# A recurrence in units of 16 value columns instead of 8, and every queue in a new order

## The chip, the cores and the metric

One core of one Trainium2 chip. The time is device microseconds of one execution, from launch to the last result. The kernel before was timed in 3 runs: median 1855.06 us, from 1853.09 to 1856.74.

## The reference

Two layers over 32 independent batches of 128 x 512 float32. The first is an attention over channels: two instance norms, two 128 x 128 projections, a softmax of 512 x 512, its product with a projection of the second input, and a residual. The second is a block in the manner of RWKV; its core is a scan over 128 time steps, in 32 heads of 16 x 16 state. It reads `x` (32 x 128 x 512) and a context of the same shape, whose rows also give the state at the start.

```
Mn = Wn @ inorm(x_c) + bn ; Mm = Wm @ inorm(x_s) + bm
A  = softmax(Mn^T Mm) ; y = Wo (Wl x_s + bl) A^T + bo + x_c
xa = ln(y) ; sx = shift(xa) - xa ; five mixes -> w, r, k, v, g
def step(s, (r_t, k_t, v_t, w_t)):
    a   = k_t[..., :, None] * v_t[..., None, :]
    out = einsum('bhi,bhij->bhj', r_t, u * a + s)
    s   = a + w_t[..., :, None] * s
x1 = y + groupnorm(out) * silu(g) @ Wo.T
out = x1 + sigmoid(xr2 @ Wfr.T) * (relu(xk2 @ Wfk.T)**2 @ Wfv.T)
```

## The kernel before, in words

Everything is float32. There is one instruction queue for each engine, written by hand: `opening()`, then `step(on)` for s = 5 to 30 (26 times, written out, not a loop on the chip), then `closing()`. A step works on five batches at once: `b0` in the attention (`att_*`), `b1` in the mixes and projections (`mid_*`), `b2` in the recurrence (`wkv_*`), `b3` in the head norm and first residual (`tail_*`), `b4` in the last products (`fin_*`). Engines meet only by semaphores; `Steps` (L53) counts labels, so the order of labels in L228 to L254 is the order in each engine's queue. TensorE's results go through rings of PSUM banks (L86 to L91): a job gets the next bank of its ring and waits, in `bank_free` (L276), for the reader of the job that had the bank last. Bank 4 (`SUM_BANK`) collects the recurrence, bank 5 (`O_BANK`) the transposed result.

The recurrence (L855 to L889) is computed for pairs of time steps. Partition = one key row of a head (128 of 512 in each of C = 4 chunks), free axis = value columns x time. A unit is one chunk and `UJ` = 8 of the 16 value columns; there are `U` = 8 units a batch. In each:

- SP loads `vrep` (`load_vrep`, L331): v of the unit, replicated over the 16 key rows of its head, from the DRAM tensor `v_dram`, 512 KB. ScalarE has stored v there (`mid_v`, L1560). `vrep` has two buffers.
- VectorE: `wkv_outer` (L862) A = vrep * kt, 8 x 126; `wkv_pair` (L868) adds each pair of A into S, 8 x 63; `wkv_scan` (L877) runs the scan over S with decays `wrep`, 8 x 64; `wkv_read` (L889) A = S * rt, each state read twice, 8 x 128. A and S have two buffers.
- GpSimd puts the state at the start into column 0 of S (`wkv_s0`, L543). Its other large jobs are the five adds of the mixes (`mid_add`, L516), `rku` and `rk2`, the power -0.5 of the head norm (`rstd_of`, L489) and the last add (`fin_out`, L556).
- TensorE: `wkv_sum` (L2168): four products of A with 32 columns of ones, 256 columns each, over the keys; four units make half of the bank.

Four more places that the change touches. In the transpose of the tanh, `mid_Wt` (L2112), 64 columns of `txn` are turned, of which 32 are those of g. `tail_xc2` (L1642) writes two scaled copies of the second norm on ScalarE, one to be shifted by a time step, and `tail_mix` (L954) adds them. The last batch goes through the same code as all others. At the start, ScalarE and TensorE wait for 14 constants (`CONSTS`).

Of the kernel before, what the change touches and what calls it, by code (L numbers as in the profile page):

```python
# [29 lines left out]
UJ = 8  # L30
U = C * HS // UJ
# [47 lines left out]
def run(step):  # L79
# [7 lines left out]
    "O:1 V:0 Tx:1 W1:1 Mn:0 Wt:1 Mm:0 Mv:1 Mw:1 S0:0 S1:0 S2:0 Vp:1 Mk:1 Mr:1 Mg:1 D1:1 S3:0 Kp:1 "  # L87
    "D2:1 E2:1 Rp:1 T0:0 T1:0 T2:0 G:1 T3:0").split())]
BACK_JOBS = [(j, int(lag)) for j, lag in (x.split(":") for x in (
    "FK:4 C:3 C2:3 FR:4 FV:4 Tg:3 Wo:3 Tx2:3").split())]  # L90
# [3 lines left out]
def build(nc, x_c, x_s, state, params, att_w, big_w, maa_w1, maa_w2, td_w1, td_w2, out, v_dram):  # L94
    with ExitStack() as ctx:
# [26 lines left out]
        w2g = sb("w2g", [2 * DM, E])  # L122
# [14 lines left out]
        rsum = sb("rsum", [P, C])  # L137
        rinv = sb("rinv", [P, C])
# [6 lines left out]
        xx = sb("xx", [P, C, P])  # L145
        tx = sb("tx", [P, P])
        txg = sb("txg", [2 * DM, P])
# [9 lines left out]
        wrep = sb("wrep", [P, C, UJ, T2])  # L157
# [10 lines left out]
        pv = sb("pv", [P, C, T2])  # L168
# [15 lines left out]
        kk = sb("kk", [P, C, P])  # L184
# [17 lines left out]
        xhat2 = sq  # L202

# [17 lines left out]
        act_setup = sem("act_setup")  # L221
        wv_centred = sem("wv_centred")
# [5 lines left out]
        dve_att = Steps(sem("dve_att"), "stats aggr nm mx0 mx1 mx2 ri1 ri0 mx3 ri2 ri3 xin xst xag nm1")  # L228
        dve_mid = Steps(sem("dve_mid"), "sx xx s0m mv mw mk mr mg s0c g")
        dve_pre = Steps(sem("dve_pre"), "kw rw")  # L230
        dve_outer = Steps(sem("dve_outer"), units("a"))
# [5 lines left out]
        act_att = Steps(sem("act_att"), "v xn yn Mn Mm p1 p2 p0 n0 n1 p3 n2 n3 T0 T1 T2 T3 xhat")  # L237
        act_mid = Steps(sem("act_mid"), "xa tn tx vT dt ez k dw r th")
# [59 lines left out]
        def _(sp):  # L298
            regs = [sp.alloc_register(f"sync_wait{i}") for i in range(2)]
            sp.dma_start(xc[:, 0, :], x_c[0]).then_inc(x_loaded[0], 16)  # L300
            sp.dma_start(xs[:, 0, :], x_s[0]).then_inc(x_loaded[0], 16)
            sp.dma_start(attw[:, :, :], att_w).then_inc(setup_loaded[0], 16)
            sp.dma_start(par[:, :], params).then_inc(setup_loaded[0], 16)
# [101 lines left out]
            def closing():  # L405
# [2172 lines left out]
```

## Time and profile before

| what | value |
|---|---|
| median of 3 runs | 1855.06 us |
| the profiled execution, its own time | 1854.93 us |
| its span, first to last instruction | 1853.2 us |
| TensorE busy | 1774.6 us, 96% |
| VectorE busy | 1744.8 us, 94% |
| ScalarE busy | 1176.3 us, 63% |
| GpSimd busy | 1015.3 us, 55% |
| chain that ended last | PE 50%, DVE 28%, issue 16%, DMA 2%, ACT 2% |
| TensorE clock, mean | 0.987 of 2.4 GHz |

In the profile PE is TensorE (PEld its weight loads, beside the matmuls), DVE VectorE, ACT ScalarE, POOL GpSimd, SP the engine that issues loads; a "q" behind a name is the engine's sequencer. `L877` is a line of the kernel. In a group's row come the line, engine, operation, result<-operands, shapes, the count, then busy us and mean ns of one, then idle time before it and what ended that. A float32 matmul is two records. Rows of the timeline begin with start and length in us; neighbours on an engine can overlap a little in the records.

### The profile page before, as it was taken

How to read it: one execution, taken by the hardware profiler on the slowest of the kernel's cores; microseconds unless marked ns; L12 is line 12 of the kernel's file. 1: busy time of each engine (PE TensorE's matmuls, PEld its weight loads, DVE VectorE, ACT ScalarE, POOL GpSimd, SP SyncE). 2: the span in 40 equal slices, each digit the busy share in tenths (PEclk: the TensorE clock that was granted, in tenths of full speed). 3: DMA queues.
4: the chain of work that ended last, by engine and by line, in shares of the span. 5: the costliest groups of instructions: out<-in, count | busy, mean ns of one | idle time of the engine just before them, and what ended most of it. 6: DMA issues, size and time to landing. Idle time of an engine off the chain costs nothing.

```text
span 1853.2 us, 35413 instructions
## 1 busy us (share of the span) xinstructions
PE 1774.6 (96%) x12420; PEld 1228.9 (66%) x12420; DVE 1744.8 (94%) x2468; ACT 1176.3 (63%) x2949; POOL 1015.3 (55%) x882
## 2 busy tenths in 40 slices
PE   5989999999999999999999999999999999999966
PEld 3666576667676667766676767666776667776743
DVE  3699999999999999999999999999999999999991
ACT  4666666666666767666667666676666666766523
POOL 1244465555665665566665566556566666554541
PEclk8999999999999999999999999999999999999978
DMA  6233434344333333433434333333343343433330
GB/s 246 72 90 96 104 85 101 89 106 105 96 88 99 99 92 104 107 91 91 104 88 107 106 97 87 98 99 93 104 108 91 90 104 86 118 96 77 93 82 18
DMA packets 81600, 180.98 MB, mean 98 GB/s; under 512 B 18288, under 2 KB 34800, under 8 KB 80400
## 3 DMA queue, kind: packets, MB, share of 16 engines
q1 hardware_dynamic: 59920, 161.93, 33.1%
q10 hardware_dynamic: 21504, 16.78, 2.8%
q8 instruction: 101, 1.65, 0.4%
q14 instruction: 75, 0.61, 0.1%
HBM read 161.91 MB, written 16.78 MB: 96 GB/s over the span
## 4 chain that ended last, share of the span: by engine, by line
PE 50%; DVE 28%; issue 16%; DMA 2%; ACT 2%; POOL 1%; DVEq 0%; ACTq 0%; POOLq 0%; SPq 0%
PE bank L2043 17%; PE bank L2050 6%; DVE A L862 6%; PE bank L2088 5%; DVE S L877 5%; PE bank L2055 4%; DVE A L889 3%; PE bank L2168 3%; DVE nmax L764 3%; DVE xf L820 3%; PE bank L2062 3%; DVE S L868 2%; PE bank L2075 2%; DMA vrep<-v_dram 2%; PE bank L2103 2%
## 5 line engine op out<-in xcount | busy, mean ns | idle before, releaser
L543 POOL COPY S<-s 128x8 f32<-128x8 f32 x256 | 190.3, 744 | 322.3 <-DVE A L889 231.6
L877 DVE TENSOR_TENSOR_SCAN S<-wrep,S 128x512 f32<-128x512 f32 x256 | 351.9, 1377 | 2.6 <-ACT wrep L1603 1.7
L889 DVE TENSOR_TENSOR A<-S,rt 128x1024 f32<-128x1024 f32 x256 | 327.5, 1283 | 0.4
L516 POOL TENSOR_TENSOR xf<-xf,xa 128x512 f32<-128x512 f32 x160 | 218.7, 1369 | 188.7 <-DVE xf L820 186.4
L862 DVE TENSOR_TENSOR A<-vrep,kt 128x1008 f32<-128x1008 f32 x256 | 310.8, 1218 | 7.4 <-DMA vrep<-v_dram 4.6
L1520 ACT ACTIVATE prob<-bank,nmax 128x512 f32<-128x512 f32 x128 | 87.4, 686 | 231.5 <-DVE nmax L764 231.5
L868 DVE TENSOR_TENSOR S<-A 128x504 f32<-128x504 f32 x256 | 225.8, 892 | 1.2
L489 POOL TENSOR_TENSOR hrs<-hrs,mhalf 128x32 f32<-128x32 f32 x32 | 198.7, 6211 | 2.7
L487 POOL TENSOR_SCALAR rstd<-mv 128x1 f32<-128x1 f32 (+1 forms) x96 | 72.8, 759 | 227.4 <-DVE mv L784 141.2
L1557 ACT ACTIVATE bank<-bank,par 128x128 f32<-128x128 f32 x640 | 174.6, 352 | 29.0 <-PE bank L2124 29.0
L2168 PE MATMUL bank<-A,slide 128*32 128x256 f32 x2048 | 163.4, 394 | 13.8 <-DVE A L889 13.4
L2075 PE MATMUL bank<-probT 128*128 128x512 f32 x256 | 132.1, 619 | 5.5 <-ACT prob L1520 2.4
L2043 PEld LDWEIGHTS bank<-xk,Wfk 128*128 128x128 f32 x1024 | 121.5, 198 | 19.5 <-DVE xk L954 18.8
L2043 PE MATMUL bank<-xk,Wfk 128*128 128x128 f32 x1024 | 127.4, 285 | 5.5 <-DVE xk L954 5.4
L1651 ACT ACTIVATE xp<-bank,prev 128x128 f32<-128x128 f32 x256 | 130.4, 509 | 0.0
L2050 PE MATMUL bank<-Wo,ogT 128*128 128x512 f32 x256 | 121.8, 620 | 7.8 <-DVE ogT L931 6.4
L2043 PEld LDWEIGHTS bank<-xf,Wr 128*128 128x128 f32 x1024 | 116.7, 192 | 18.9 <-POOL xf L516 16.2
L2043 PE MATMUL bank<-xf,Wr 128*128 128x128 f32 x1024 | 121.9, 277 | 5.3 <-ACT prob L1520 5.3
L2043 PEld LDWEIGHTS bank<-xf,Wv 128*128 128x128 f32 x1024 | 116.9, 192 | 14.3 <-POOL xf L516 11.9
L2043 PEld LDWEIGHTS bank<-xf,Wk 128*128 128x128 f32 x1024 | 116.8, 192 | 14.0 <-issue 12.1
L2043 PE MATMUL bank<-xf,Wv 128*128 128x128 f32 x1024 | 122.6, 278 | 0.7 <-POOL xf L516 0.7
L2043 PE MATMUL bank<-xf,Wk 128*128 128x128 f32 x1024 | 122.5, 278 | 0.3
(143 smaller groups left out, 3890.8 us busy)
## 6 DMA issues: line engine op xcount, KB each, us to landing
vrep<-v_dram SPq DMA_DIRECT2D x256, 512.0 KB
xc<-x_c SPq DMA_DIRECT2D x32, 256.0 KB, 6.2
xs<-x_s SPq DMA_DIRECT2D x32, 256.0 KB, 9.4
v_dram<-vT ACTq DMA_DIRECT2D x32, 256.0 KB, 7.2
out<-rr ACTq DMA_DIRECT2D x32, 256.0 KB, 6.4
st<-state SPq DMA_DIRECT2D x64, 2.0 KB, 6.4
Wv<-big_w SPq DMA_DIRECT2D x1, 1024.0 KB, 7.2
Wk<-big_w SPq DMA_DIRECT2D x1, 1024.0 KB, 9.2
```

Source lines behind the costliest of these rows:

```text
L489: po.tensor_tensor(rs, rs, mhalf[:, 0:rs.shape[1]], ALU.pow).then_inc(own.sem, 1)
L516: po.tensor_tensor(xf[:, b, :, :], xf[:, b, :, :], xa[:, :, 1:P + 1], ALU.add).then_inc(pool_mid.sem, 1)
L543: po.tensor_copy(S[:, u % 2, :, 0], s0[:, p, k:k + UJ]).then_inc(pool_wkv.sem, 1)
L862: ve_.tensor_tensor(A[:, u % 2, :, 0:P - 2], vrep[:, u % 2, :, 0:P - 2], k, ALU.mult).then_inc(dve_outer.sem, 1)
L868: ve_.tensor_tensor(S[:, u % 2, :, 1:T2], first(a), second(a), ALU.add).then_inc(dve_pair.sem, 1)
L877: ve_.tensor_tensor_scan(s, wrep[:, u % C, :, :].rearrange("p j t -> p (j t)"), s, 0.0, ALU.mult, ALU.add).then_inc(dve_scan.sem, 1)
L889: ve_.tensor_tensor(out4, s, r, ALU.mult).then_inc(dve_read.sem, 1)
L1557: last = sc.activation(ps, ps, ACT.Identity, bias=col("maa_stack", c, MIX.index(f)))
L2043: last = pe.matmul(ps[:, o * P:(o + 1) * P], w[:, c, o * P:(o + 1) * P], src[:, c, :], start=(c == 0), stop=(c == C - 1))
L2050: last = pe.matmul(bank_of(job)[:, :], src[:, c, :], w[:, c, :], start=(c == 0), stop=(c == C - 1))
L2075: pe.matmul(bank_of(f"S{t}")[:, :], Mn[:, t * P:(t + 1) * P], Mm, start=True, stop=True).then_inc(pe_att.sem, 1)
L2168: last = pe.matmul(bank[SUM_BANK][32 * g:32 * g + 32, 2 * P * half:2 * P * (half + 1)], ones, A[:, u % 2, g:UJ:4, :], start=(c == 0), stop ...
```

## The change

Units are now one chunk and all 16 value columns: `U` = 4. The replicated v still comes in halves of `WJ` = 8 columns (`V` = 8 loads), one buffer for each half. So per batch there are 8 outers, 4 pair sums of twice the size, 8 scans in 4 pairs, 4 read-outs of twice the size, 4 seed copies of 16 columns, and 4 sums of 512 columns. S has one buffer. `xx` now lies in `xhat`, `kk` in `xk2`, `pv` in `rk2`. The transpose that holds g takes 96 columns instead of 64. All queues have a new order; r, g, Tx2 and FK are computed at the front of the next step. The last batch has code of its own: the head norm's root on ScalarE and a reciprocal on VectorE, the shifted copies of the second norm on VectorE, FK in four banks, FV, the product and the last add in halves, the add on VectorE, and two stores. The start loads the attention weights first, and waits for fewer constants.

```diff
-UJ = 8
-U = C * HS // UJ
+UJ = 16
+U = C
+WJ = 8
+V = 2 * U
-        vrep = sb("vrep", [P, 2, UJ, P])
+        vrep = sb("vrep", [P, 2, WJ, P])
-        S = sb("S", [P, 2, UJ, T2])
+        S = sb("S", [P, UJ, T2])
...
             def wkv_outer(n, m, p, v):
+                u, half = v // 2, v % 2
+                eng.wait_ge(vrep_loaded[half], 16 * (n * U + u + 1))
...
+                if half == 0:
+                    eng.wait_ge(pe_wkv.sem, pe_wkv.count(f"r{(u - 2) % U}", n if u >= 2 else n - 1))
...
             def wkv_pair(n, m, p, u):
+                eng.wait_ge(dve_outer.sem, dve_outer.count(f"a{2 * u + 1}", n))
+                eng.wait_ge(dve_read.sem, dve_read.count(f"q{(u - 1) % U}", n if u else n - 1))
...
             def wkv_scan(n, m, p, u):
...
+                for j in range(0, UJ, WJ):
+                    s = S[:, j:j + WJ, :].rearrange("p j t -> p (j t)")
+                    last = ve_.tensor_tensor_scan(s, w, s, 0.0, ALU.mult, ALU.add)
+                last.then_inc(dve_scan.sem, 1)
...
             def wkv_s0(n, m, p, u):
-                v1 = held(eng, regs[1], dve_read.count(f"q{(u - 2) % U}", n if u >= 2 else n - 1))
+                v1 = held(eng, regs[1], dve_read.count(f"q{(u - 1) % U}", n if u >= 1 else n - 1))
...
             def wkv_rk2(n, m, p):
-                eng.wait_ge(pe_tail.sem, pe_tail.count("C2", n - 1))
+                eng.wait_ge(dve_tail.sem, dve_tail.count("ob", n - 1))
...
             def wkv_sum(n, m, p, u):
+                    last = pe.matmul(bank[SUM_BANK][32 * g:32 * g + 32, :], ones, A[:, u % 2, g:UJ:4, :],
+                                     start=(u == 0), stop=(u == C - 1))
...
             def mid_Wt(n, m, p):
-                pe.transpose(bank_of("Wt")[0:2 * DM, P:2 * P], txn[:, P - DM:P + DM], ident[:, :])
+                pe.transpose(bank_of("Wt")[0:3 * DM, P:2 * P], txn[:, 2 * DM:5 * DM], ident[:, :])
...
             def tail_gn(n, m, p):
+                if n == NB - 1:
+                    eng.wait_ge(last_sd, 1)
+                    ve_.reciprocal(hrs[:, :], hrs[:, :]).then_inc(last_rs, 1)
...
             def tail_mix(n, m, p, i):
+                    for c in range(C):
+                        last = ve_.tensor_scalar(xp2[:, i, c, 1:P + 1], bank[SUM_BANK][:, c * P:(c + 1) * P],
+                                                 prev[:, i, 0, c:c + 1], prev[:, i, 1, c:c + 1], ALU.mult, ALU.add)
...
             def fin_y(n, m, p):
+                        ve_.tensor_tensor(rr[:, y], (bank_of("FV"), bank[O_BANK])[half][:, y], rr[:, y], ALU.mult).then_inc(last_y, 1)
+                        eng.wait_ge(last_y, half + 1)
+                        ve_.tensor_tensor(rr[:, y], rr[:, y], x1[:, y], ALU.add).then_inc(last_out, 1)
```

The new order of a step on the engines that matter here (one batch's jobs shortened; `M` mixes, `P` projections):

```
VectorE: pair b3 3; ag b4; scan b3 3; xin, xst b1; s0c b2; rstd b4; xag b1; kw b2; outer b2 0; read b3 3;
  outer b2 1; mix b4 0; rstd1 b1; stats, aggr b0; pair b2 0; mix b4 1; scan b2 0; o b3; gate b2; rstd b0;
  outer b2 2; shift b1; o2 b3; rw b2; xx b1; ob b3; outer b2 3; read b2 0; var b3; max b0 0; pair b2 1;
  max 1; scan b2 1; mix b1 0; max 2; rinv 0; read b2 1; rinv 1; mix b1 1; max 3; outer b2 4, 5; gn b3;
  rinv 2; mix b1 2; y b4; rinv 3; mix b1 3, 4; s0 b1; gate b3; pair, scan b2 2; outer b2 6; read b2 2;
  outer b2 7; x1, st b3
GpSimd: s0 b3 3; add b2 3; rstd b4; add b2 4; rstd1 b1; s0 b2 0; ez2 b2; xa0 b1; rstd b0; rk, rk2 b2; s0 b2 1;
  hrs b3; s0 b2 2; add b1 0; xc20 b3; add b1 1, 2; out b4
TensorE: O b1; P r b2; Tx2 b4; V b0; P g b2; FK b4; Tx b1; C b3; sum b3 3; C2 b3; FR b4; Mn, Mm b0; To b3; W1 b1;
  S0; Wt b1; S1, S2; M v,w b1; FV b4; S3; sum b2 0, 1; M k,r,g b1; P v b1; Tg b3; D1 b1; P k b1; T0; Wo b3; T1, T2;
  D2 b1; sum b2 2; T3
ScalarE, from the last bias on: scale b0 0; oT b3; scale 1, 2, 3; vT b1 and its store; k b1; probT 0; dt b1; ...
```

## Rows read from the trace of the kernel before

**Rows 1.** source L774, 600 to 1000 us: count, ns min/median/max, first and last start

```profile
L774 DVE SCALAR_TENSOR_TENSOR xin<-bank,bo,xc x8: 735/740/744, 616.0 to 999.7; 128x512 f32<-128x512 f32 x8
```

**Rows 2.** windows: stretch, length, busy PE, PEld, DVE, ACT, POOL, clock, DMA share, GB/s

```profile
616.00:999.70 383.70, 381.97 (x2724) 265.95 (x2716) 381.51 (x540) 256.20 (x646) 228.61 (x189) 1.00 0.37 98
...
674.00:678.00 4.00, 4.00 (x34) 3.66 (x33) 3.83 (x9) 2.94 (x6) 2.75 (x4) 1.00 0.53 154
```

**Rows 3.** chain of waits from 616 to 735 us: start, us, what

```profile
646.65 1.22 DVE A L889
...
656.20 3.81 PE bank L2043 x32
...
660.01 0.57 PE bank L2168 x8
...
662.04 3.57 PE bank L2043 x32
...
677.68 3.44 PE bank L2050 x8
```

**Rows 4.** sources L868, L877, L889 from 616 to 1383 us: ns min/median/max

```profile
L868 DVE TENSOR_TENSOR S<-A x112: 667/682/1749, 623.9 to 1382.1; 128x504 f32<-128x504 f32 x112
...
L877 DVE TENSOR_TENSOR_SCAN S<-wrep,S x112: 1202/1217/2207, 622.2 to 1378.6; 128x512 f32<-128x512 f32 x112
...
L889 DVE TENSOR_TENSOR A<-S,rt x112: 1208/1216/1832, 626.6 to 1381.0; 128x1024 f32<-128x1024 f32 x112
```

**Rows 5.** VectorE's groups from 616 to 999.7 us: busy us, mean ns, idle before

```profile
L877 DVE TENSOR_TENSOR_SCAN S<-wrep,S 128x512 f32<-128x512 f32 x56 | 78.8, 1408 | 0.8 <-ACT wrep L1603 0.7
...
L889 DVE TENSOR_TENSOR A<-S,rt 128x1024 f32<-128x1024 f32 x56 | 72.4, 1293 | 0.0
...
L868 DVE TENSOR_TENSOR S<-A 128x504 f32<-128x504 f32 x56 | 51.5, 929 | 0.2
```

**Rows 6.** timeline from 691.5 to 704 us: start, length in us, engine, line

```profile
692.02 0.68 DVE L923 TENSOR_TENSOR oc<-bank,hrs 128x512 f32<-128x512 f32 x1
...
692.11 2.46 POOL L516 TENSOR_TENSOR xf<-xf,xa 128x512 f32<-128x512 f32 x2
...
692.62 0.68 DVE L820 TENSOR_TENSOR xf<-bank,sx 128x512 f32<-128x512 f32 x1
...
701.45 1.22 DVE L889 TENSOR_TENSOR A<-S,rt 128x1024 f32<-128x1024 f32 x1
...
701.61 2.09 POOL L516 TENSOR_TENSOR xf<-xf,xa 128x512 f32<-128x512 f32 x1 [3.67 <-DVE xf L820]
...
702.58 2.20 DVE L877 TENSOR_TENSOR_SCAN S<-wrep,S 128x512 f32<-128x512 f32 x1
```

**Rows 7.** GpSimd's seed copy and mix add from 616 to 1383 us: ns min/median/max

```profile
L543 POOL COPY S<-s x112: 197/801/1210, 628.0 to 1382.3; 128x8 f32<-128x8 f32 x112
...
L516 POOL TENSOR_TENSOR xf<-xf,xa x70: 1179/1186/2096, 637.3 to 1367.3; 128x512 f32<-128x512 f32 x70
```

**Rows 8.** timeline of the end

```profile
1812.69 5.46 POOL L489 TENSOR_TENSOR hrs<-hrs,mhalf 128x32 f32<-128x32 f32 x1
...
1822.05 5.40 PE L2050 MATMUL bank<-Wo,ogT 128*128 128x512 f32 x8 [2.39 <-DVE ogT L931]
...
1848.70 0.69 DVE L959 TENSOR_TENSOR rr<-bank,rr 128x512 f32<-128x512 f32 x1 [9.87 <-PE bank L2050]
...
1850.77 0.34 ACTq L1677 DMA_DIRECT2D out<-rr  x1
```

**Rows 9.** timeline of the start

```profile
18.31 0.69 DVE L764 TENSOR_REDUCE nmax<-bank 128x1 f32<-128x512 f32 x1
```

**Rows 10.** timeline, tile v_dram: v's store, the first outer, the landing

```profile
644.44 0.37 ACTq L1568 DMA_DIRECT2D v_dram<-vT  x1
...
667.33 1.19 DVE L862 TENSOR_TENSOR A<-vrep,kt 128x1008 f32<-128x1008 f32 x1
...
DMA to landing us min/median/max: 6.3/6.6/7.5
```

More of the change, by code:

```diff
@@ L202, in build @@
         xhat2 = sq
+        xx = by_chunk(xhat[:, :])
+        kk = xk2
+        pv = rk2
         def col(name, c, f=0):
@@ L1277, in step @@
[L1277 to L1297 removed]
+                wkv_outer(*b2, 7)
@@ L1648, in tail_xc2 @@
                     ps = bank_of("Tx2")[:, c * P:(c + 1) * P]
[L1649 to L1652 removed]
+                    last = sc.activation(dst[:, c, :], ps, ACT.Identity,
+                                         bias=here[:, i, 1, c:c + 1], scale=here[:, i, 0, c:c + 1])
@@ L1674, in fin_store @@
             def fin_store(n, m, p):
-                eng.wait_ge(pool_fin.sem, pool_fin.count("out", n))
-                dst = out[n] if isinstance(n, int) else out[bass.ds(n, 1)].rearrange("o p f -> (o p) f")
-                eng.dma_start(dst, rr[:, :]).then_inc(out_stored, 16)
+                if n < NB - 1:
+                    eng.wait_ge(pool_fin.sem, pool_fin.count("out", n))
+                    eng.dma_start(out[n], rr[:, :]).then_inc(out_stored, 16)
+                else:
+                    for half in range(2):
+                        y = slice(half * E // 2, (half + 1) * E // 2)
+                        eng.wait_ge(last_out, half + 1)
+                        eng.dma_start(out[n][:, y], rr[:, y]).then_inc(out_stored, 16)
             def opening():
@@ L2215, in tail_Tx2 @@
                 transposes("Tx2", lambda c: xhat2[:, c * P:(c + 1) * P]).then_inc(pe_tail.sem, 1)
+                if n == NB - 1:
+                    for c in range(C):
+                        last = pe.transpose(bank[SUM_BANK][:, c * P:(c + 1) * P], xhat2[:, c * P:(c + 1) * P], ident[:, :])
+                    last.then_inc(last_tx, 1)
             def tail_FK(n, m, p):
@@ L2219, in tail_FK @@
                 eng.wait_ge(*bank_free("FK", n))
-                proj_T("FK", W["Wfk"], xk2).then_inc(pe_tail.sem, 1)
+                if n < NB - 1:
+                    proj_T("FK", W["Wfk"], xk2).then_inc(pe_tail.sem, 1)
+                else:
+                    for o in range(C):
+                        for c in range(C):
+                            last = pe.matmul(bank[o][:, 0:P], W["Wfk"][:, c, o * P:(o + 1) * P],
+                                             xk2[:, c, :], start=(c == 0), stop=(c == C - 1))
+                        last.then_inc(pe_tail.sem if o == C - 1 else last_fk, 1)
             def fin_FR(n, m, p):
@@ L2227, in fin_FV @@
             def fin_FV(n, m, p):
-                eng.wait_ge(act_fin.sem, act_fin.count("kk", n))
-                eng.wait_ge(*bank_free("FV", n))
-                proj_N("FV", W["Wfv"], kk).then_inc(pe_fin.sem, 1)
+                if n < NB - 1:
+                    eng.wait_ge(act_fin.sem, act_fin.count("kk", n))
+                    eng.wait_ge(*bank_free("FV", n))
+                    proj_N("FV", W["Wfv"], kk).then_inc(pe_fin.sem, 1)
+                else:
+                    eng.wait_ge(*bank_free("FV", n))
+                    for half in range(2):
+                        col2 = slice(half * E // 2, (half + 1) * E // 2)
+                        for c in range(C):
+                            if half == 0 and c < C - 1:
+                                eng.wait_ge(last_kk, c + 1)
+                            elif half == 0:
+                                eng.wait_ge(act_fin.sem, act_fin.count("kk", n))
+                            last = pe.matmul((bank_of("FV"), bank[O_BANK])[half][:, col2], ogT[:, c, :], W["Wfv"][:, c, col2],
+                                             start=(c == 0), stop=(c == C - 1))
+                        last.then_inc(pe_fin.sem if half else last_fv, 1)
             def opening():
```

1618 lines of the change are left out of this document (760 added, 858 removed).

## The prediction

> **What bounds the kernel now.** I read the windows first. In the steady stretch, which is 26 written-out steps of one batch each, one instruction that runs once a batch (`xin`) comes 8 times from 616.0 to 999.7 us [rows 1]: 383.7 / 7 = 54.8 us a batch. In that stretch VectorE is busy 381.5 of 383.7 us and TensorE 382.0 [rows 2]. The reader should see that two engines are full at once; ScalarE (67%) and GpSimd (60%) are not. Then the chain of waits: it changes between long unbroken TensorE pieces and VectorE stretches inside each batch [rows 3], so a gain on one engine alone would be worth little. A busy VectorE is not all work: its groups have means well over their medians [rows 4, 5]. Scan: mean 1408 ns against a median of 1217; pair sum: 929 against 682; read-out: 1293 against 1216. With 8 of each per batch the excess is 8 x (0.19 + 0.25 + 0.08) = 4.1 us of 54.8. The timeline shows what it is: the GpSimd add issued at 701.61, while the read-out runs, takes 2.09 us instead of 1.18 and then holds up the scan, which takes 2.20 instead of 1.22 [rows 4, 6, 7]. At 692.11 the same adds run beside VectorE work whose operand is in PSUM and nothing stretches [rows 6]. So the floors, the busy times per batch, are 382.0 / 7 = 54.6 us for TensorE (matmul ends are modelled, so a little less is work: I take 54.5) and 381.5 / 7 = 54.5 for VectorE, of which 50.4 is its own work.
>
> A rule of the Trainium skill, in "SBUF — State Buffer", section "SBUF: two separate sides", says the same: the pair of ports that VectorE and GpSimd share is an exclusive lock, held for the whole instruction, by a VectorE instruction with two SBUF inputs. Rows 6 agree (2.20 against 1.22 us). The rule speaks against this change in one point: a read-out twice as long keeps GpSimd out 2.2 us instead of 1.1. By it alone GpSimd would get up to 1 us later at 4 places a batch, which its 40% of idle time holds.
>
> **The change part by part.**
>
> *VectorE, merged units.* Per batch the pair sums go from 8 x 504 to 4 x 1008 elements and the read-outs from 8 x 1024 to 4 x 2048; outers and scans stay 8 and 8. So 8 instruction heads go. Their price from durations: 1216 - 682 = 534 ns for 520 more elements is 1.03 ns each, leaving 0.16 us of fixed time [rows 4]. Their price from starts: the instruction of 692.02 is followed at 692.62, 0.60 us for 512 elements, leaving 0.07 [rows 6]. Bounds 8 x 0.07 = 0.6 and 8 x 0.16 = 1.3 us; I take 0.6, as starts are what an engine without gaps pays (own estimate from these rows).
>
> *VectorE against GpSimd.* Four of the eight seed copies go (0.20 us alone, by the shortest one; the median of 0.80 is waiting [rows 7]). What they do to VectorE is at most 4 x 0.2 = 0.8 us, at least 0. The new orders move the large GpSimd jobs. Walking both queues with the durations above: the adds of v, w, k and the final add (2.29 us with its wait) now follow, on VectorE, a stretch of PSUM work (`gn`, three mixes, `fin_y`), and the adds of r and g are put off past `x1` and the statistics into the next step. Of before's 4.1 us some 2.1 should be left: about 0.5 each from `rku`, `rk2` and the g add, and 0.6 from small ones. The bounds: 0 gained (4.1 stays) to 2.6. I take 1.3, the middle, since the walk is good to a us.
>
> VectorE's floor: 54.5 - 0.6 - 1.3 = 52.6; without the second term 53.9.
>
> *TensorE.* A unit's sum is 0.57 us now, and what follows it is longer: the projection behind matmuls of its own tile shape takes 3.57, one behind a change of shape 3.81 [rows 3]. So 0.2 more per change of shape. A record of 512 columns is 3.44 / 8 = 0.43 us, so 256 columns are 0.21; the new unit has twice the columns: 0.57 + 2 x 0.21 = 1.0. Raw: 8 x 0.57 = 4.6 becomes 4.0, 0.6 us less. Shape changes: in the step there are nine now (seven around sums, two mix products that stand alone); in the new order four (sum 3; mix v,w; sums 0 and 1 with the other mix products behind them; D2 with sum 2). 5 x 0.2 = 1.0. The 96-column transpose is a full-width tile by its shape where the 64-column one was a shape of its own; the latter sat beside a sum, so it is in the count. Without it the new order would have a tenth change: 0.2. Floor: 54.5 - 1.6 = 52.9. Bounds: 0.6 (only raw) to 1.8.
>
> By the Trainium skill ("TensorEngine Tiling (Array Packing)", section "Key Properties") changing the tiling mode drains TensorE; the 3.81 against 3.57 us is that, in this kernel. It gives no figure that the sum uses.
>
> *New waits.* S has one buffer and its seed copy must come between read-out u-1 and scan u. On VectorE a pair sum (1.1) and one or more 0.6 us instructions stand between them; the copies are queued on GpSimd in front of the power of `hrs` (5.46 us and more [rows 8]) for u = 1, and for u = 2 scan 2 comes some 16 us after the variance that starts it. I take 0. Where that cover goes, the scan waits up to 1.2 us (the longest copy [rows 7]), and behind it on VectorE its read-out, and on TensorE the unit's sum. `rk2` now waits for `ob` of the batch before, as it shares its buffer with `pv`; behind it on GpSimd is the seed copy of unit 1, which waits for read-out 0 anyway, and that follows `ob` on VectorE: 0. The other shared buffers (`xx` in `xhat`, `kk` in `xk2`) wait for TensorE jobs of the batch before: 0. Rp, G, Tx2 and FK go to the front of the next step, where O, `xin` and xk2 are ready at about the place where they are now; 0, at the worst their own order on TensorE costs VectorE 0.8 (the first maximum behind FR, Mn, Mm, To and W1). SP still issues 8 replicated loads of 512 KB a batch, each when the outer two before it is done; x and state loads move among them: 0.
>
> *Steady period.* Floors 52.9 and 52.6; before, the period was 0.3 over its floors. For the TensorE order above and the v trip, both of about the same length, I take twice that: 53.5: 1.3 us less. 26 steps: 34 us. The six batches of opening and closing, where TensorE and VectorE are less full, get 0.7 each: 4 us.
>
> *The end.* The power for the last head norm runs 1812.69 to 1818.15 and holds `gn` [rows 8]. It becomes an add, ScalarE's root and a reciprocal, about 1.1 us with hops; but FR of batch 30 (3.4 us) now stands in front of the transposes, and Tg is behind FV in both: 10 us from the last sum to Tg become about 8. 2 us. xk2 gets its shifted half on VectorE: 3.0 us of ScalarE become 1.4 + part of 1, and the mix starts 1.3 earlier. The last y, add and store: 1848.70 to 1850.77 is 2.1 us; in halves on VectorE 0.4 + 0.4 + hops = 0.9, 1.2 us less. The split of FK and of relu and square hides behind FR as now: 0. Together 4.5; 3 to 8: Wo took 5.40 us at 1822.05, in a stretch after TensorE had stood idle, where the same 8 records take 3.44 at 2.4 GHz in mid-run [rows 3, 8]; with shorter idle time before it up to 2 us more come back.
>
> *The start.* ScalarE no longer waits for all constants and head scales before it normalises. But the first maximum waits at 18.31 for the centring of Wv, which waits for its transfer [rows 9]. Only what the second and third maximum waited comes back: 1.5 us; 0 to 4.
>
> Sum: 34 + 4 + 4.5 + 1.5 + 2 for waits of the first batches, where both engines still have gaps (own estimate, 0 to 5) = 46. The profiled execution took 1854.93 us (span 1853.2, 1.7 around it), against a median of 1855.06: the same. 1855 - 46 = 1809 us.
>
> **Rivals.**
>
> A. *Only the heads count.* The GpSimd lock costs what it did: VectorE's floor 53.9, period 54.2, 0.6 us less: 26 x 0.6 = 16, plus 2 and 6 for the ends: 1831 us. For it: GpSimd's large jobs are all still there, and where they meet VectorE depends on tenths of a us. Against: the new queue puts three of five adds and the final add beside PSUM work. The Trainium skill's lock rule from above, at its full length, is this rival too: longer read-outs, so fewer but longer refusals.
>
> B. *Both floors are reached, and the walk undersold the lock.* Period 52.9: 26 x 1.9 = 49, plus 6 and 8: 1792 us.
>
> C. *The v trip decides; slower.* v goes to DRAM and comes back replicated. Now its store is issued at 644.44 and lands 6.6 us later, and the outer product that needs it starts at 667.33 [rows 10]: about 10 us of cover, taking 6.1 us for issue and landing of the replicated load (estimate: 512 KB at the 154 GB/s of 674 to 678 us [rows 2] is 3.4 us, plus 2 and the issue). In the new ScalarE order vT stands behind `oT` and all four scales. From the end of read-out 1: sum 1.1, mixes 1.1, Vp 3.8, Tg 0.5, oT 1.5, scales 2.0, vT 0.6, trip 6.6 + 0.6 + 5.5 = 23.3 us. VectorE's work from there to the next outer 0 is 21.9, and 24 to 25 with its waits. So some 1 us of cover is left of 10. Each us that the path is longer than my figures, beyond that one, is a us per batch on VectorE; the kernel is slower from 2.3 us more on. At 3 us more: period 55.5, 26 x 0.7 = 18, less 6 at the ends: 1867 us. For it: transfers queue behind each other on SP. Against: the DMA share is 38%.
>
> D. *Nothing.* The new orders cost in waits what the heads save: 1850 to 1856.
>
> **How the numbers follow.** Main case 0.53, 1795 to 1825; A 0.2; B 0.12; C 0.1; D 0.05. What a measurement can tell from no change is about 0.2%, 3.7 us. Faster: 0.53 + 0.2 + 0.12 = 0.85; same 0.04; slower 0.11. The range takes in A with its spread and most of B: 1786 to 1848.
>
> **What would show it.** The windows: period 53.5, TensorE and VectorE both over 98%. Pair sum of 1008 elements 1.2 us and read-out of 2048 2.3 us at the median, and a mean of the scan near 1.25; if the scan's mean stays near 1.4, A. Unit sums: 8 records spaced 1.0 us; projections behind them 3.8, the others 3.57. If VectorE's outer waits for `vrep`, C. At the end `gn` 2 us after the variance. The forecast is wrong if the period is over 54.4 or a releaser not named here holds VectorE or TensorE over 1 us a batch.

## The result, and the profile after

The changed kernel takes 1784.86 us (median of 4 runs, 1782.70 to 1785.45) against 1855.06: ratio 0.9615, 95% interval 0.9604 to 0.9626, 70 us less. The forecast was 1809 us, range 1786 to 1848: the sign and the place were right, the size was not, and the time lies 1 us under the range. The profiled execution of the changed kernel took 1785.44 us, its span is 1783.7.

The shares of the chain of waits by engine, from the profile's page. TensorE holds 84% of it, where it held 50% before:

```profile
PE 84%; DVE 10%; issue 3%; ACT 1%; POOL 1%; DMA 0%; SPq 0%; DVEq 0%; POOLq 0%; ACTq 0%
```

The once-a-batch instruction `xin` in the whole run, and the window that covers six of its intervals (the stretch of [rows 1, 2]; columns as in [rows 2]):

```profile
L765 DVE SCALAR_TENSOR_TENSOR xin<-bank,bo,xc x32: 723/725/751, 34.7 to 1640.8; 128x512 f32<-128x512 f32 x32
...
640.10:955.30 315.20, 315.20 (x2139) 224.88 (x2138) 303.47 (x416) 220.06 (x552) 183.45 (x139) 1.00 0.39 102
```

315.2 / 6 = 52.5 us a batch against 54.8. Over the whole run the mean interval is (1640.8 - 34.7) / 31 = 51.81 us; before, `xin` ran from 35.0 to 1709.7, 54.02 us. So the 31 intervals gave 68.6 of the 70 us, start and end nearly nothing. The reader should see that two full engines have become one: TensorE is busy 315.20 of 315.20 us, VectorE 50.6 us a batch, 1.9 under it. Rows 2 had both at 54.5.

VectorE's groups in this window, which answer to [rows 4, 5]:

```profile
L855 DVE TENSOR_TENSOR A<-vrep,kt 128x1008 f32<-128x1008 f32 x48 | 58.0, 1217 | 0.5
L873 DVE TENSOR_TENSOR_SCAN S<-wrep,S 128x512 f32<-128x512 f32 x49 | 57.3, 1209 | 0.2
L885 DVE TENSOR_TENSOR A<-S,rt 128x2048 f32<-128x2048 f32 x24 | 54.7, 2278 | 0.0
L863 DVE TENSOR_TENSOR S<-A 128x1008 f32<-128x1008 f32 x24 | 28.7, 1195 | 0.0
L811 DVE TENSOR_TENSOR xf<-bank,sx 128x512 f32<-128x512 f32 x30 | 20.3, 676 | 7.6 <-PE bank L2113 3.8 <-PE bank L2011 3.8
...
L962 DVE TENSOR_TENSOR xk<-xk,xp 128x512 f32<-128x512 f32 x6 | 6.5, 1083 | 0.5
```

The scan's mean is 1209 ns: it was 1408, with a median of 1217. None of the four large groups stretches any more; a small rest is left in the mix of xk (last row), whose mean is 1083 ns where it was 680, 0.4 us a batch. The row of L811 is the first place where VectorE waits for TensorE, 1.3 us a batch. Where the stretching went, the timeline of one batch shows (start, length, engine):

```profile
671.04 0.67 DVE L811 TENSOR_TENSOR xf<-bank,sx 128x512 f32<-128x512 f32 x1
671.32 1.18 POOL L534 TENSOR_TENSOR xf<-xf,xa 128x512 f32<-128x512 f32 x1
671.62 0.68 DVE L755 TENSOR_REDUCE nmax<-bank 128x1 f32<-128x512 f32 x1
672.22 2.47 DVE L855 TENSOR_TENSOR A<-vrep,kt 128x1008 f32<-128x1008 f32 x2
673.59 2.14 POOL L534 TENSOR_TENSOR xf<-xf,xa 128x512 f32<-128x512 f32 x1
675.29 0.67 DVE L811 TENSOR_TENSOR xf<-bank,sx 128x512 f32<-128x512 f32 x1
```

The add of 671.32 runs beside VectorE work that reads a bank (PSUM), and neither is longer. The add of 673.59 meets the outer products, and now GpSimd is the one that waits (2.14 instead of 1.18 us), and no engine in this profile waits for that.

The chain from 668 us on (start, us, what) answers to [rows 3]:

```profile
669.57 0.86 PE bank L2043 x2
670.43 1.85 PE bank L2135 x16
672.28 1.10 PE bank L2092 x24
673.38 3.77 PE bank L2011 x32
677.15 0.44 PE bank L2023 x4
677.59 0.89 PE bank L2113 x8
678.48 3.57 PE bank L2011 x32
```

TensorE's pieces follow without a break; sums 0 and 1 stand together (1.85 us), the mixes with the same tile shape behind them, and only the projection after them is longer (3.77 against 3.57).

### The profile page after: what moved, and what is told of

Its sections match the earlier page's. It is cut to its first block, busy times and chain, and to the rows that moved or that the text cites. A ratio compares the mean times of both kernels' runs of the same rounds, so it can differ in the third digit from the quotient of the medians.

```text
span 1783.7 us, 32768 instructions
## 1 busy us (share of the span) xinstructions
PE 1718.5 (96%) x11408; PEld 1218.0 (68%) x11408; DVE 1638.8 (92%) x2224; ACT 1184.9 (66%) x2954; POOL 955.0 (54%) x752
## 4 chain that ended last, share of the span: by engine, by line
PE 84%; DVE 10%; issue 3%; ACT 1%; POOL 1%; DMA 0%; SPq 0%; DVEq 0%; POOLq 0%; ACTq 0%
PE bank L2011 29%; PE bank L2018 17%; PE bank L2135 6%; PE bank L2043 5%; PE bank L2056 5%; PE bank L2023 5%; PE bank L2092 4%; PE bank L2030 3%; DVE S L873 2%; PE bank L2071 2%; DVE A L885 2%; PE bank L2113 1%; PE bank L2146 1%; DVE A L855 1%; PE bank L2036 1%
## 5 line engine op out<-in xcount | busy, mean ns | idle before, releaser
L560 POOL COPY S<-s 128x16 f32<-128x16 f32 x128 | 81.8, 639 | 409.5 <-DVE A L885 409.4
L873 DVE TENSOR_TENSOR_SCAN S<-wrep,S 128x512 f32<-128x512 f32 x256 | 299.8, 1212 | 1.2 <-issue 0.2
L885 DVE TENSOR_TENSOR A<-S,rt 128x2048 f32<-128x2048 f32 x128 | 291.7, 2279 | 0.1
L503 POOL TENSOR_TENSOR hrs<-hrs,mhalf 128x32 f32<-128x32 f32 x31 | 176.8, 5704 | 2.6
L552 POOL TENSOR_TENSOR rk<-rT,kT 128x256 f32<-128x256 f32 x32 | 106.0, 3313 | 103.3 <-DVE oc L910 103.3
L863 DVE TENSOR_TENSOR S<-A 128x1008 f32<-128x1008 f32 x128 | 155.8, 1218 | 0.2
L811 DVE TENSOR_TENSOR xf<-bank,sx 128x512 f32<-128x512 f32 x160 | 108.1, 676 | 44.6 <-PE bank L2011 22.5
L2135 PE MATMUL bank<-A,slide 128*32 128x512 f32 x1024 | 131.7, 605 | 2.5 <-DVE A L885 2.4
L503 POOL TENSOR_TENSOR rstd<-rstd,mhalf 128x1 f32<-128x1 f32 (+1 forms) x96 | 123.8, 1289 | 8.0
L1471 ACT ACTIVATE probT<-bank 128x512 f32<-128x512 f32 x128 | 72.4, 593 | 80.6 <-PE bank L2023 80.5
```

The costliest lines, as they stand in the source:

```text
L503: po.tensor_tensor(rs, rs, mhalf[:, 0:rs.shape[1]], ALU.pow).then_inc(own.sem, 1)
L863: ve_.tensor_tensor(S[:, :, 1:T2], first(a), second(a), ALU.add).then_inc(dve_pair.sem, 1)
L873: last = ve_.tensor_tensor_scan(s, w, s, 0.0, ALU.mult, ALU.add)
L885: ve_.tensor_tensor(out4, s, r, ALU.mult).then_inc(dve_read.sem, 1)
L2135: last = pe.matmul(bank[SUM_BANK][32 * g:32 * g + 32, :], ones, A[:, u % 2, g:UJ:4, :], start=(u == 0), stop=(u == C - 1))
```

## The experiments

Seventeen kernels were timed beside the kernel before, one of them the changed kernel once more. The ratios to it compare them across chips. "Interval" is the mean distance of `xin` over 31 intervals; the busy shares are of 1000 to 1500 us. The changed kernel and the runs whose loop is the same or nearly so (after again, e3, e7, e8, e12) have intervals from 51.80 to 51.88 us, so a difference of less than 0.1 us is not told from nothing.

| kernel | us | ratio, 95% | interval | TensorE | VectorE |
|---|---|---|---|---|---|
| before | 1855.1 | 1 | 54.02 | 99.5% | 99.4% |
| after, again | 1786.5 | 0.9616, 0.9601-0.9630 | 51.88 | 100% | 96.3% |
| after (profile of the first run) | 1784.9 | 0.9615, 0.9604-0.9626 | 51.81 | 100% | 96.5% |
| e6 merge, old order | 1916.5 | 1.0315, 1.0285-1.0345 | 55.66 | 96.4% | 95.1% |
| e1 new order, all split | 1794.4 | 0.9660, 0.9645-0.9674 | 52.17 | 100% | 96.9% |
| e4 VectorE's part split | 1791.1 | 0.9642, 0.9627-0.9656 | 51.92 | 100% | 97.1% |
| e2 two shape changes more | 1793.7 | 0.9655, 0.9639-0.9671 | 52.07 | 100% | 95.7% |
| e3 64-column transpose | 1785.0 | 0.9622, 0.9607-0.9637 | 51.80 | | |
| e10 two adds moved back | 1801.9 | 0.9712, 0.9697-0.9726 | 52.35 | 98.9% | 96.7% |
| e5 two head sums more | 1815.2 | 0.9796, 0.9770-0.9822 | 52.69 | 98.8% | 96.9% |
| e5 three | 1853.4 | 0.9979, 0.9967-0.9991 | 53.86 | 97.5% | 96.6% |
| e5 four | 1922.1 | 1.0363, 1.0346-1.0380 | 55.99 | 96.6% | 93.6% |
| e14 two reductions, at waits | 1789.2 | 0.9644, 0.9629-0.9658 | 51.87 | 100% | 98.6% |
| b1 before, GpSimd's adds cut | 1835.5 | 0.9901, 0.9884-0.9919 | 53.50 | 100% | 95.2% |
| b2 before, 16 products less | 1853.1 | 0.9984, 0.9974-0.9994 | 53.92 | 96.2% | 99.1% |
| b3 both | 1807.5 | 0.9744, 0.9729-0.9758 | 52.55 | 98.9% | 97.4% |
| e7 ends off | 1786.7 | 0.9623, 0.9609-0.9637 | 51.80 | | |
| e8 root first | 1780.5 | 0.9593, 0.9579-0.9607 | 51.80 | | |
| e12 end reordered | 1777.4 | 0.9573, 0.9559-0.9586 | 51.80 | | |

**Merge or order?** e6 puts the merged units, buffers and shared storage into the queues of before:

```diff
-UJ = 8
+UJ = 16
 # queues of before; of wkv_pair/scan/read/sum/s0 every second call goes
-                wkv_pair(*b2, 4)
                 wkv_pair(*b2, 5)   ->  wkv_pair(*b2, 2)
```

> The kernel before with the merged work of the change alone: units of 16 value columns, half-unit buffers of vrep, one S, the storage put to second use; every queue keeps its old order, the transpose stays at 64 columns and the ends are the old ones. Theory 1 (the new order takes the GpSimd collisions away and with them most of the gain): the collisions stay, about 4.1 us per batch; the merge itself gives at most the 0.6 us of heads on VectorE and 0.8 to 1.8 us on TensorE, period 54.2, in all 1836 us, 1825 to 1845. Theory 2 (the bigger units bring the gain): 1785 to 1800.

It is 3.2% slower than before: both theories fell. One view tells why; TensorE's waits and what released them (total, times, longest), in e6 and, behind it, in the kernel before:

```profile
PE bank L2061 <- DVE A L867: 77.7, 65, 7.5
```

```profile
PE bank L2168 <- DVE A L889: 13.4, 12, 2.8
```

A sum can start only when the doubled read-out is through, and in the old order it is next in TensorE's queue: 64 us more of waiting, for 61 us more of time. So the merge does not pay in the old order, with each merged call about where its second half stood; no other place for it in that order was tried. e1 is the reverse, the new order with all merged instructions cut back:

```diff
-                ve_.tensor_tensor(S[:, :, 1:T2], first(a), second(a), ALU.add)
+                for j in range(0, UJ, WJ):      # read-out, seed copy alike
+                    last = ve_.tensor_tensor(S[:, j:j + WJ, 1:T2], first(a), second(a), ALU.add)
...
+                for h in range(2):              # the sum: 2 x 256 columns, adjacent
```

> The changed kernel with the queues as they are, but every merged instruction of the recurrence cut back in two that stand side by side: pair, read-out and seed copy of 8 columns each, the sum as two times 256 columns. Buffers, transpose and ends stay as changed. Theory 1 (the order decides; TensorE runs without a gap and the two halves of a sum are adjacent, so no change of tile shape comes back; VectorE has about 1.9 us to spare per batch): 1785 to 1790 us. Theory 2 (fewer instruction heads are the gain): 0.6 to 1.3 us per batch come back, 1804 to 1826.

Ratio 0.9660: 62 of 70 us remain without any merged instruction. The merge is worth 8 us, 0.36 us an interval; that lies between the two theories. e4 splits only pair sum and read-out.

> The changed kernel with only the pair and the read-out of VectorE cut back in two of 8 columns each: 8 more VectorE instructions per batch, about 0.5 to 0.6 us. Theory 1 (TensorE alone sets the period, VectorE has 1.9 us to spare): 1785 to 1786 us. Theory 2 (VectorE counts as well, or both are coupled as the prediction took it): +0.55 x 32 = 18 us, 1803.

The interval grew by 0.11 us over the first profile of the changed kernel and by 0.04 over the second (0.9642, some 5 us, at the edge of what the runs tell from nothing); the time lies between the theories, nearer the first. VectorE's busy time rose by 0.44 us a batch (50.42 from 49.98, its share times the interval): the price of heads by starts, 0.6, was nearer than that by durations, 1.3.

**TensorE's shape changes.** e2 swaps two calls, e3 takes the transpose back.

```diff
-                att_S(*b0, 3)
                 wkv_sum(*b2, 0)
+                att_S(*b0, 3)
                 wkv_sum(*b2, 1)
```

> The changed kernel with one head product of 512 columns set between the two adjacent 32-row sums 0 and 1 of TensorE's queue in the loop, so that TensorE changes its tile shape twice more per batch; no instruction more or less. Theory 1 (a change of shape costs TensorE about 0.2 us each and TensorE has no gap to hide it): +0.3 to 0.4 us per batch, 1793 to 1797 us. Theory 2 (a change of shape is free or hidden): 1785 to 1786.

> The changed kernel with the 64-column transpose and the second layer of mix g at rows 32 to 63 of its weights, as before; all else as changed. Theory 1 (a part of mix g in the 32-row tile behind the other mixes costs a different tile position and little else): +0.1 to 0.3 us per batch, 1788 to 1794 us. Theory 2 (the 96 columns save nothing): 1785.

In the chain of e2 the 1.85 us for two adjacent sums are apart:

```profile
669.46 0.99 PE bank L2135 x8
670.45 1.06 PE bank L2043 x2
671.51 1.00 PE bank L2135 x8
```

0.99 + 1.06 + 1.00 against 0.86 + 1.85: 0.34 us in this place; the interval grew by 0.26 (0.19 against the second profile), 0.1 to 0.13 us a change. The transpose is worth nothing measurable.

**The collisions.** e10 moves only GpSimd's adds of r and g back behind `fin_out`.

```diff
-                mid_add(*b2, 3)
                 tail_rstd(*b4)
-                mid_add(*b2, 4)
...
                 fin_out(*b4)
+                mid_add(*b1, 3)
+                mid_add(*b1, 4)
```

> The changed kernel with GpSimd's two long additions of the mixes r and g set back to the place they had before, behind the store of the last result in its loop. Nothing else is moved. Theory 1 (what the new order won is that GpSimd's additions no longer fall on VectorE's outer products and scans; but VectorE has 1.9 us to spare): VectorE's busy time rises by 1 to 2 us per batch, the time by 0 to 10 us. Theory 2 (each microsecond of collision is paid in full): +1.2 to 2 us per batch, 1823 to 1850. If neither the busy time nor the time moves, the additions' place did not matter.

It fell between the two: +0.0097, 18 us. VectorE's group from 640 to 955 us and, behind it, TensorE's:

```profile
L863 DVE TENSOR_TENSOR S<-A 128x1008 f32<-128x1008 f32 x24 | 34.5, 1437 | 0.0
```

```profile
L2135 PE MATMUL bank<-A,slide 128*32 128x512 f32 x192 | 24.3, 601 | 3.2 <-DVE A L885 3.2
```

The pair sum's mean went from 1195 to 1437 ns: one of four a batch waits 1 us for an add. TensorE then waits 0.53 us a batch for the read-out behind it. The interval grew by 0.54 us: the price was half of the collision, not nothing, although VectorE is idle 1.9 us a batch in the changed kernel.

**Is VectorE's 1.9 us slack?** e5 repeats a head sum (0.67 us) in place:

```diff
+                for i in range(2):          # 3, 4
+                    ve_.tensor_reduce(hvar[:, :], heads(sq[:, :]), X, ALU.add)
...
                 ve_.tensor_reduce(hvar[:, :], heads(sq[:, :]), X, ALU.add)
```

> The changed kernel with the sum of squares per head (128x512, 0.67 us) computed two times more per batch on VectorE: +1.45 us per batch of VectorE work with its waits, 52.1 us against TensorE's 52.5. Theory 1 (TensorE alone sets the period, VectorE has 1.9 us to spare): 1785 to 1790 us. Theory 2 (the two are coupled, a period is some 0.6 us over the nearer floors): 1795 to 1805. Theory 3 (VectorE sets it): +46 us, 1831.

> The same with four times more: +2.9 us of VectorE work per batch, 53.5 us against TensorE's 52.5. Theory 1 (the larger of the two floors is the period): +1.0 us per batch, 1817 us, 1812 to 1825. Theory 2 (coupled): 1830 to 1840. Theory 3 (VectorE set it already): +93 us, 1878.

> The changed kernel with three more head sums per batch, between the runs with two (1815 us, a TensorE pause of 0.6 us per batch, no fall of the clock) and four (1922 us, a pause of 2.1 us per batch, behind it the value product takes 6.5 instead of 3.6 us). Theory 1 (a pause costs itself while the granted clock stays full, and only a longer one costs the clock as well): the pause is about 1.3 us; with the clock kept 1838 us, with the clock lost behind it 1880 to 1920. Theory 2 (cost in proportion to the extra work): 1868, half way, with a clock between the two.

None came out by the larger floor alone: two more cost 30 us, between theories 2 and 3, four more 137 us, beyond all; three lie 15 us over theory 1 with the clock kept and far under the clock lost each time. With four, one batch reads (timeline, in order of cause):

```profile
643.47 2.83 DVE L915 TENSOR_REDUCE hvar<-sq 128x32 f32<-128x512 f32 x4
...
646.94 0.68 DVE L755 TENSOR_REDUCE nmax<-bank 128x1 f32<-128x512 f32 x1
647.66 0.69 ACT L1462 ACTIVATE prob<-bank,nmax 128x512 f32<-128x512 f32 x1 [2.31 <-DVE nmax L755]
648.54 1.69 PE L2095 MATMUL bank<-tx,w 32*128 32x128 f32 x16 [2.06 <-issue]
650.16 6.50 PE L2021 MATMUL bank<-Wfv,xk 128*128 128x512 f32 x8
```

The four extra sums and the kernel's own fifth stand ahead of the maximum. The maximum waits behind the sums, the exponential for the maximum, and the mix product for the bank that the exponential reads: it starts 0.1 us after it. (The profile puts this wait down to "issue".) The same place in the changed kernel has no pause: the exponential's accumulator read ends at 664.53 and the product starts at 664.78. So of 1.9 us of idle VectorE only what lies ahead of this maximum helps here: 0.44 us. TensorE's idle time ahead of this product is, over what the changed kernel has, 0.6 us a batch with two sums more, 1.2 with three, 1.9 with four (2.06 in this batch). And then TensorE's value product takes 6.50 us, where it takes 3.6. The windows before and behind the pause show the granted clock (the third number from the right):

```profile
644.50:648.54 4.04, 1.98 (x8) 0.70 (x6) 3.94 (x6) 1.47 (x6) 1.34 (x2) 1.00 0.30 65
648.54:656.70 8.16, 8.16 (x25) 4.30 (x26) 7.23 (x10) 3.92 (x13) 5.89 (x5) 0.58 0.00 1
```

So a pause of 2.06 us costs a second time: over the 8.2 us behind it the granted clock is 0.58, most of it at the lower level of 1.2 GHz. A record of the value product has a mean of 604 ns in the changed kernel and with two more sums; with three it is 672 and with four 841. From 1000 to 1500 us the mean granted clock is 1.00, 0.99 and 0.96 with two, three and four. The steps in time are +30 us for the first two sums, +38 for the third and +69 for the fourth.

e14 adds as much VectorE work as the first of these, but ahead of the two mixes at which VectorE waits for TensorE:

```diff
             def mid_mix(n, m, p, i):
+                if i >= 3:
...
+                    ve_.tensor_reduce(early[:, :], w2[:, :], X, ALU.add)
                 eng.wait_ge(act_mix.sem, act_mix.count(f"b{f}", n))
```

> The changed kernel with two more VectorE reductions of 128x512 (0.68 us each) per batch, as many as in the run with twice the extra head sums (1815 us, VectorE busy 51.1 of 52.7), but set directly ahead of the two mixes (r and g) at which VectorE waits 0.64 us each for TensorE. Theory 1 (what decides is whether the work stands before a wait of its engine, not its sum): 1785 to 1790 us. Theory 2 (what decides is the sum of VectorE's work per batch): 1810 to 1818.

1789 us against 1815, with VectorE's busy share even higher (98.6%), and an interval of 51.87 us, within what the changed kernel itself shows. The place decides, not the sum. The timeline shows the idle 0.64 us filled:

```profile
677.04 0.66 DVE L812 TENSOR_REDUCE early<-w 128x1 f32<-128x512 f32 x1
677.75 0.69 DVE L815 TENSOR_TENSOR xf<-bank,sx 128x512 f32<-128x512 f32 x1
678.36 0.68 DVE L812 TENSOR_REDUCE early<-w 128x1 f32<-128x512 f32 x1
679.08 0.69 DVE L815 TENSOR_TENSOR xf<-bank,sx 128x512 f32<-128x512 f32 x1
```

**Which engine held the kernel before?** Each relief alone, then both:

```diff
-                po.tensor_tensor(xf[:, b, :, :], xf[:, b, :, :], xa[:, :, 1:P + 1],    # b1
+                po.tensor_tensor(xf[:, b, :, 0:2], xf[:, b, :, 0:2], xa[:, :, 1:3],
...
+                used = C - 1 if job in ("Vp", "Kp") else C                             # b2
```

> The kernel before with GpSimd's five additions of the mixes cut to 2 of 128 columns per chunk (most of the addition is left out), so that they can hardly fall on VectorE's instructions; nothing else is changed. In the kernel before TensorE is busy 53.8 of 54.0 us per batch and VectorE 53.7. Theory 1 (both engines stand at their floor, so relief of one alone is stopped by the other): 0 to 8 us faster, 1847 to 1855. Theory 2 (the collisions are the loss, and taking them away is the gain of the change): 1.5 to 3 us less per batch, 1760 to 1807.

> The kernel before with the last of four contraction chunks left out of the k and the v projection: 16 matrix products of about 0.117 us less per batch, TensorE 1.87 us shorter; nothing else is changed. Theory 1 (both engines at their floor): VectorE's 53.7 us hold the period, 0 to 9 us faster, 1846 to 1855. Theory 2 (TensorE alone bounds the kernel before): 1.87 x 32 = 60 us, 1795.

> Both reliefs at once in the kernel before: GpSimd's additions cut, 16 matrix products less. Theory 1 (the two engines' relief is worth much only together): 1.8 to 1.9 us less per batch, some 58 us faster, 1795 to 1805, far more than the sum of the two alone. Theory 2 (the effects add up): the sum of the two single gains.

Both leave out work that the result needs, so they only tell what time is worth where. Alone they give 18 us (0.9901) and 3 us (0.9984); together 47 (0.9744), more than the sum, but less than the 58 that I expected (1807 us, outside 1795 to 1805). In b1 TensorE is the wall (500.00 of 500 us busy) and VectorE's outer products wait for it:

```profile
L862 DVE TENSOR_TENSOR A<-vrep,kt 128x1008 f32<-128x1008 f32 x256 | 327.5, 1283 | 54.0 <-PE bank L2168 50.6 <-DMA vrep<-v_dram 1.8
L877 DVE TENSOR_TENSOR_SCAN S<-wrep,S 128x512 f32<-128x512 f32 x256 | 324.6, 1271 | 5.1 <-ACT wrep L1603 5.0
```

b1 lies between its two ranges; my bound of 8 us was too low: TensorE's busy time itself fell by 0.26 us a batch (53.76 to 53.50), beside its 0.26 us of gaps. Even b3 keeps 1% of TensorE idle, which the changed kernel's order does not.

**The end.** e7 takes the last batch's own code out, e8 moves its root, e12 moves more.

```diff
-                if n < NB - 1:              # e7, at every such place
+                if n < NB:
...
+                last_root()                 # e8, ScalarE, and e12
                 fin_rr(*at(30))
...
+                tail_To(*at(31))            # e12, TensorE
                 fin_FR(*at(30))
-                tail_To(*at(31))
-                fin_FV(*at(30))
                 tail_Tg(*at(31))
+                fin_FV(*at(30))
```

> The changed kernel with the special last batch taken out: no table load and root on ScalarE, no work moved to idle engines, no halves; the last batch uses GpSimd's power function and one store as all others, in the new order of the queues. Theory 1 (from the last 32-row sum to the end the trace shows 44.4 us with the special code against 44.2 before, so it brings nothing): 1785 to 1786 us, within 1 us. Theory 2 (the prediction's sum: about 4.5 us of savings, given back by the new order of the queues ahead of it): 1789 to 1790.

> The changed kernel with the root of the last batch set ahead of the two tanh of the batch before it in ScalarE's closing queue: its table is then there, the tanh table is loaded behind it, and the root no longer waits for two tanh and a table load. Theory 1 (the chain of waits: the normalized output of the last batch starts at 1750.6 us behind tanh 1747.3 to 1748.5, a table load of 1.28 us and the root; the sums of squares are there at 1744.5 and TensorE's Wo of the last batch could start by that much earlier): 3 to 4 us faster, 1781 to 1782. Theory 2 (the tanh of batch 30 then comes late and its result holds TensorE or the stores at the end): 1784 to 1787.

> The kernel with the early root (1780.5 us), and in the closing part the transposes of the last normalized output set ahead of the receptance product of batch 30, the transposes of the gated input ahead of the value product of batch 30, and on VectorE and ScalarE the gate and its scaling ahead of batch 30's result. Theory 1 (the chain of waits at the end runs through the sums of squares, the root and Wo of the last batch; Wo starts 1.4 us or more earlier, and without TensorE's pause of 2.8 us ahead of it may run at 3.6 instead of 5.4 us): 1777 to 1779 us. Theory 2 (the bank that Wo needs is read by batch 30's result only then, and Wo starts no earlier): 1780 to 1782.

In time e7 is hardly told from the changed kernel (0.9623 against 0.9615 and 0.9616). The profiles say more. From the end of the last sum to the end of the span it is 44.1 us before (1853.2 - 1809.1), 44.4 in the changed kernel (1783.7 - 1739.3) and 46.8 in e7 (1785.5 - 1738.7). So the new order of the queues costs the end 2.7 us, and the code for the last batch wins 2.4 of them back. Little of that comes from the root: the normalized output `oc` starts 11.9 us behind the last sum in e7, after GpSimd's power, 11.2 in the changed kernel (at 1750.57), and 9.2 in the kernel before. In the chain of e7:

```profile
1745.04 5.47 POOL hrs L503
...
1750.61 0.70 DVE oc L924
```

The chain of the changed kernel shows what eats the gain of the root (answers to [rows 8]):

```profile
1739.33 3.63 PE bank L2018 x8
1742.96 0.44 PE bank L2162 x4
...
1747.91 0.63 ACT rr L1634
...
1748.56 1.28 ACT L1573
...
1749.86 0.24 ACT hrs L1573
...
1754.74 5.74 PE bank L2018 x8
```

Batch 30's product FR (3.63 us) stands ahead of the transposes, and the root waits behind batch 30's tanh, its scaling and a table load of 1.28 us. The timeline of ScalarE shows that this load is the third in 5.4 us: the code loads the root's table early, the tanh of batch 30 puts its own in its place, and the root has to load again.

```profile
1744.49 1.28 ACT L1569 ACT_TABLE_LOAD   x1
...
1745.99 1.28 ACT L1630 ACT_TABLE_LOAD   x1
...
1748.56 1.28 ACT L1573 ACT_TABLE_LOAD   x1
```

Wo starts at 1754.74 after a TensorE pause and takes 5.74 us. e8 gives 6 us against e7, which was timed beside it; by the profiles 2.4 of them are the last batch's code, which e8 keeps, and 3.6 the early root (40.8 us behind the last sum against 44.4). e12 gives 9.1 us against the changed kernel beside it, 1777.4 us: the fastest here. Its chain has Wo at

```profile
1748.63 3.69 PE bank L2017 x8
```

From the end of the last sum to the end of the span it is 38.1 us (1775.3 - 1737.2). While its Wo runs, TensorE's clock is granted in full (1.00); while e8's Wo runs it is 0.69, with 5.40 us for the same eight records.

## Why the prediction was wrong in size

The forecast missed by 24 us, and two steps failed. In the sum it is *Steady period*: over the floors I set a distance, "I take twice that: 53.5". The kernel before shows 0.3, the doubling rests on no row, and in the changed kernel nothing of it is there: TensorE's idle time in the window is 0.00 us and the period is TensorE's busy time, 52.5. Of the 1.0 us between 53.5 and 52.5 that distance is 0.6 and TensorE's floor, put at 52.9, 0.4: 26 us in 26 steps. The period also fell more in the opening than I took, and the end and the start, overrated by 6 us together, hide a part of the miss.

The mechanism behind the missing distance is the second step, *VectorE against GpSimd*: "The bounds: 0 gained (4.1 stays) to 2.6. I take 1.3". VectorE's busy time fell from 54.5 to 50.6 us a batch, 3.9; 0.4 to 0.6 of it are heads, so 3.3 to 3.5 of the 4.1 us are collisions gone, above the upper bound. (My own walk had said 2.0, and I took less.) It had left about 0.5 us each for `rku`, `rk2` and the g add. `rk2` does take 3.9 us in the steady batches, but it is GpSimd that waits there, while VectorE's outer product (658.52, 1.19 us) and read-out (659.64, 2.27 us) keep their lengths:

```profile
658.74 3.89 POOL L552 TENSOR_TENSOR rk<-rT,kT 128x256 f32<-128x256 f32 x1 [3.99 <-DVE oc L910]
```

The walk counted each meeting as VectorE's loss; a meeting costs the engine that comes second. The Trainium skill ("SBUF — State Buffer", "SBUF: two separate sides") says that whichever instruction starts first gets the pair of ports for its whole length. The timeline at 673.59 agrees (2.14 us for 1.18, the outer products unchanged); the prediction had used that rule for a longer wait of GpSimd at the read-outs, but not in its walk. It is not always GpSimd that waits behind a VectorE run: at 701.61 in [rows 6] the add gets in between read-out and scan, and in e10 before a pair sum. What decides whether it gets in between two VectorE instructions is not shown.

How the two steps hang together, three runs show in part. e10 puts one collision of 1 us a batch back, and TensorE is idle 0.6 us a batch: the distance that I had forecast. With two head sums more it is 0.65, in b3 0.6. e14 leaves VectorE less room than any of these (98.6% busy) and has no distance. So the distance comes from VectorE being late at one place, and its busy time alone does not bring it; whether a floor of 52.6 would have brought it in the new order stays open.

*TensorE.* Predicted -1.6, measured -2.0 (54.5 to 52.5). By parts: the merged sum 0.25 (e1 less e4, for 0.6), a shape change 0.13 (e2, for 0.2), the transpose 0 (e3, for 0.2). These make 5 x 0.13 + 0.25 = 0.9. Of the other 1.1, 0.26 fit what b1 took off by freeing the collisions alone; the rest is spread over groups that each became about 0.1 us shorter and stays open. As TensorE alone sets the period now, about half of the steady gain is without a shown cause.

*VectorE, merged units.* Taken at 0.6; measured 0.44.

*New waits*: none cost anything that shows. The seed copies wait for the read-out only, and the outer products 0.5 us in six batches.

*The end*: predicted 4.5 (3 to 8), measured -0.3 (44.1 to 44.4 us behind the last sum). The 10 us from the last sum to the transposes Tg, forecast at 8, became 12.0 (1739.3 to 1751.3). I had named FR's place but neither the table loads nor batch 30's tanh ahead of the root. *The start*: 0.3 for 1.5. *Waits of the first batches*: the seven first intervals gained 2.8 us each (`xin` of batch 7 from 397.1 to 377.5), the 24 after them 2.05, so the opening had 5 us of its own, for the 2 taken.

*Rivals.* A falls: the scan's mean is 1209 ns. B, with 1792 us, was nearest; but it had both engines at their floors, and what came is TensorE alone at its own. Its chance was put at 0.12. C falls: v's store lands after 3.1 us (median of the whole run; 7.2 before), and no outer product waits for it.

*Signs.* As forecast came the pair sum (1.20 us), the read-out (2.28), the scan's mean (1.21), the sums (0.93 to 1.0 us a unit) and the projections (3.77 and 3.57). The period of 53.5 and VectorE over 98% did not, nor `gn` 2 us after the variance: it starts 6 us after it. Two TensorE results that the prediction had not named hold VectorE 0.6 us a batch each at L811, 1.3 together; beside a full TensorE that costs nothing.

What the whole says of the 70 us: b2 and b3 show that the same relief of TensorE is worth 3 us alone and 29 once GpSimd's additions are out of the way; e1 shows that 62 us come without any merged instruction. How they divide between collisions and shape changes can't be said in parts that add up, since each counts only when the other engine makes room.

## What to carry to other kernels

Where two engines are both over 99% busy, ask for what relieves both, and test the pair: the reliefs here gave 18 and 3 us alone and 47 together. Idle time of an engine is slack only ahead of the instruction where it idles; the same 1.3 us of extra work a batch cost 30 us in one place and at most some 5 in another. Put GpSimd's long instructions beside VectorE work that reads PSUM, or at the end of a VectorE run that such work follows, so that GpSimd is the one to wait. At the end of a kernel, follow the chain across the batch before: a table load or an older product ahead of the last root undoes code written for it. A table that is loaded early helps only if nothing that needs another table runs in between.

## What the runs showed of the hardware

A TensorE pause of 2.06 us once in 56 us brought the granted clock down to 0.58 in the 8.2 us behind it, and a product from 3.6 to 6.5 us. With a pause of 0.6 us a batch the clock stayed at 1.00 and the product's records at 604 ns; the interval grew by 0.88 us, 0.65 of it idle time of TensorE. The Trainium skill's page "TensorE: Matmul & The Clock Gate" ("What's actually happening") tells that the clock falls to half when TensorE has been idle; the windows agree, at a pause that in the kernel's total (TensorE 96.6% busy) looks harmless. ScalarE's table load took 1.28 us each time, with the next instruction 0.01 to 0.02 us behind it.
